# VectorE's row order, a TensorE transposition in tile 0 and the place of the second value rows, in a fused decoder layer

## What is computed

```python
x = x + _L0_attn_ref(_layernorm(x, axis=-1), L0_attn_W_qkv, L0_attn_W_out, L0_attn_b_out)
x = x + _L0_xattn_ref(_layernorm(x, axis=-1), ctx_1024, ctx_1024, mask_Bx1xSxS2_ik1, ...)
x = x + _L0_ffn_ref(_layernorm(x, axis=-1), L0_ffn_w1, L0_ffn_b1, L0_ffn_w2, L0_ffn_b2)
# self attention, in blocks of 128 rows
scores = jnp.where(causal, jnp.einsum('bnqd,bnkd->bnqk', blk(q), blk(k)) * scale, -jnp.inf)
p = jnp.exp(scores - max); p = p / (sum(p) + 1e-06); out = p @ blk(v) @ W_out.T + b_out
# cross attention
scores = jnp.where(mask == 0, NEG_INF, q @ k.T * SCALE); out = (silu(scores) @ v) @ Wo.T
```

## Time and profile before

| | before |
|---|---|
| median of 3 runs | 1257.65 us |
| profiled execution, device time | 1257.62 us |
| its span, first to last instruction | 1255.8 us |
| PE / DVE / ACT / POOL busy | 98% / 56% / 39% / 20% |
| mean granted TensorE clock | 0.994 |

### The profile page before, as it was taken

How to read it: one execution, slowest core, us unless ns; L and a number is a source line. 1 busy time by engine, 2 the same in 40 slices (tenths; PEclk the granted TensorE clock), 3 DMA queues, 4 the chain that set the end, 5 groups by cost and what they waited for, 6 DMA issues and landing times.

```text
span 1255.8 us, 15452 instructions
## 1 busy us (share of the span) xinstructions
PE 1230.2 (98%) x5560; PEld 1019.8 (81%) x5560; DVE 700.8 (56%) x1266; ACT 489.6 (39%) x888; POOL 254.1 (20%) x226
## 2 busy tenths in 40 slices
PE   9979999999999999999999999999999999999998
PEld 7867878787878788878888888888888888888887
DVE  8777878887888876855733433424424333334211
ACT  7336464646464648453332232222222222323221
POOL 2223232323232332159402001001001020010000
PEclk9999999999999999999999999999999999999999
DMA  8451515151515140325120010020100200100000
GB/s 298 148 138 33 156 35 155 33 158 36 153 34 154 38 118 13 126 92 178 50 67 1 1 68 1 1 67 0 64 3 0 67 0 0 67 0 0 35 1 33
DMA packets 76789, 82.22 MB, mean 65 GB/s; under 512 B 8257, under 2 KB 47169, under 8 KB 76737
## 3 DMA queue, kind: packets, MB, share of 16 engines
q1 hardware_dynamic: 68672, 77.90, 20.0%
q10 hardware_dynamic: 8064, 3.67, 1.3%
HBM read 48.51 MB, written 18.35 MB: 53 GB/s over the span
## 4 chain that ended last, share of the span: by engine, by line
PE 55%; DVE 0%; issue 0%; DVEq 0%
PE bank L54 18%; PE bank L55 18%; PE bank L56 18%; DVE resid L1403 0%; DVEq L1402 0%
## 5 line engine op out<-in xcount | busy, mean ns | idle before, releaser
L1393 DVE TENSOR_TENSOR hid_lo<-gelu_out,hid_hi 128x512 fp32r<-128x512 f32 x128 | 97.3, 760 | 405.0 <-ACT gelu_out L1357 405.0
L1353 ACT ACTIVATE hid_hi<-bank,small 128x512 fp32r<-128x512 f32 x128 | 88.0, 688 | 499.2 <-PE bank L56 499.2
L54 PE MATMUL bank<-zT,w_parts 128*128 128x512 f32 x656 | 255.5, 389 | 1.7 <-DVE zT L864 0.9
L56 PE MATMUL bank<-zT,w_parts 128*128 128x512 f32 x656 | 255.3, 389 | 0.0
L55 PE MATMUL bank<-zT,w_parts 128*128 128x512 f32 x656 | 255.3, 389 | 0.0
L54 PE MATMUL bank<-w2p_hi,hid_lo 128*128 128x512 f32 x512 | 199.3, 389 | 0.0
L55 PE MATMUL bank<-w2p_lo,hid_hi 128*128 128x512 f32 x512 | 199.3, 389 | 0.0
L56 PE MATMUL bank<-w2p_hi,hid_hi 128*128 128x512 f32 x512 | 199.2, 389 | 0.0
L54 PEld LDWEIGHTS bank<-zT,w_parts 128*128 128x128 f32 x656 | 123.1, 188 | 28.1 <-issue 2.6
L55 PEld LDWEIGHTS bank<-zT,w_parts 128*128 128x128 f32 x656 | 123.2, 188 | 25.4
L56 PEld LDWEIGHTS bank<-zT,w_parts 128*128 128x128 f32 x656 | 123.1, 188 | 25.5
(11 more groups left out here) (156 smaller groups left out, 2039.9 us busy)
## 6 DMA issues: line engine op xcount, KB each, us to landing
x_in<-in_x SPq DMA_DIRECT2D x32, 256.0 KB, 4.8
x_dram<-resid SPq DMA_DIRECT2D x32, 256.0 KB, 2.4
raws<-in_w SPq DMA_DIRECT2D x32, 256.0 KB, 3.2
resid<-x_dram SPq DMA_DIRECT2D x32, 256.0 KB, 3.7
out_dram<-resid SPq DMA_DIRECT2D x32, 256.0 KB, 2.1
raws<-in_x SPq DMA_DIRECT2D x28, 256.0 KB, 3.5
z_cols<-raws SPq DMA_DIRECT2D x112, 64.0 KB, 2.0
z_cols<-scratch SPq DMA_DIRECT2D x56, 64.0 KB, 2.1
```

Source lines behind the costliest of these rows:

```text
L54: pe.matmul(out_ap, lhs[1], rhs[0], start=start, stop=False)
L56: return pe.matmul(out_ap, lhs[0], rhs[0], start=False, stop=stop)
L1353: act.activation(hid[0][:, c % 4, :], bank[4 + c % 3][:, :], ACT.Gelu, bias=b1_col[:, c:c + 1])
L1393: dve.tensor_tensor(hid[1][:, c % 4, :], gelu_out[:, c % 2, :], f(hid[0][:, c % 4, :]), ALU.subtract).then_inc(hid_lo, 1)
```

## The change

It does three things, and what goes with them.

1. DVE in a step: `rows_ahead` and `mask_now` stand ahead of `start_step` in every step from 1 (the mask in step 7 too); then `q_low` 0 to 2, `values_low`, `q_low` 3. GpSimd's bias adds now wait in every step from 1 to 6 for the keys' low parts (`kv_ready`).
2. Tile 0's second normalisation is transposed by TensorE: 16 transposes into banks 7, 5, 0, 1 behind `y_rows` 1 of tile 1, evacuated by ACT and DVE. Its `turn2` and 16 DMAs go. DVE makes tile 1's z1 low parts (`z1_low`) ahead of tile 0's second statistics.
3. TensorE in a step: value rows 1 stand in front of the self scores, in step 0 too, with their wait for the third masked score.

```diff
+FIRST_Z2_BANK = (7, 5, 0, 1)
@@ sync, step
-                            if more(a):
-                                sp.wait_ge(z2_turned, NB * (a + 1))
+                            if more(a) and not first(a):
+                                sp.wait_ge(z2_turned, NB * a)
                                 move_squares(sp, scratch, range(QUADS // 2), z2_moved)
@@ gpsimd, step
-                                if b is not None and first(b):
-                                    pool.wait_ge(kv_ready, HEADS_PER_CHUNK)
+                                if b is not None:
+                                    pool.wait_ge(kv_ready, len(BLOCKS) * b + HEADS_PER_CHUNK)
@@ scalar, step
+                                if first(a):
+                                    for i in range(NB):
+                                        act.wait_ge(z2T_done, i + 1)
+                                        act.activation(attn[0][:, :, cols(i)], chunks(bank[FIRST_Z2_BANK[i]][:, :]),
+                                                       ACT.Copy).then_inc(z2T_hi, 1)
@@ vector, step
-                                if first(b):
+                                if more(a):
                                     rows_ahead(a + 1, b)
-                                    mask_now(b)
+                                mask_now(b)
                                 start_step(b)
-                                if more(a) and not first(b):
-                                    rows_ahead(a + 1, b)
-                                q_low(b, 0)
-                                q_low(b, 1)
-                                if not first(b):
-                                    mask_now(b)
-                                q_low(b, 2)
-                                if not first(b):
-                                    values_low(b)
+                                for m in range(EC - 1):
+                                    q_low(b, m)
+                                values_low(b)
                                 q_low(b, EC - 1)
                                 dve.wait_ge(mask_ready, b + 1)
                                 for j in range(3):
                                     mask_scores(b, j)
-                                if first(b):
-                                    values_low(b)
@@ vector, after the first residual
+                            if first(a):
+                                for c in range(EC):
+                                    z1_low(1, c)
@@ tensor, step
                             value_rows(0)
+                            if b is not None:
+                                pe.wait_ge(s2_masked, PAIRS * b + 3)
                             pe.wait_ge(y_lo, EC * (a + 1))
+                            value_rows(1)
...
-                            if b is not None:
-                                pe.wait_ge(s2_masked, PAIRS * b + 3)
-                            value_rows(1)
@@ tensor, y_rows of the next tile
                                 for m in range(EC):
                                     y_rows(a + 1, m)
+                                    if first(a) and m == 1:
+                                        pe.wait_ge(keys_out, EC)
+                                        for i in range(NB):
+                                            transposed_rows(pe, z2_ready, a, i, FIRST_Z2_BANK[i], z2T_done)
```

More of the change, by code:

```diff
@@ L642, in last_step @@
                         def last_step(b):
-                            sp.wait_ge(z2_moved, MOVES * (TILES - 1))
+                            sp.wait_ge(z2_moved, MOVES * (TILES - 2))
                             for c in range(STAGES):
@@ L774, in step @@
                                     z1_high_now(a + 1)
-                                act.wait_ge(z2_turned, NB * (a + 1))
-                                move_squares(act, scratch, range(QUADS // 2, QUADS), z2_moved)
+                                if not first(a):
+                                    act.wait_ge(z2_turned, NB * a)
+                                    move_squares(act, scratch, range(QUADS // 2, QUADS), z2_moved)
                                 y_high(a + 1, 0)
                                 y_high(a + 1, 1)
-                                act.wait_ge(z2_moved, MOVES * (a + 1))
-                                for c in range(EC):
-                                    act.activation(by_blocks(attn[0], c), by_quads(c), ACT.Copy).then_inc(z2T_hi, 1)
+                                if first(a):
[3 more added lines that the diff above has]
+                                                       ACT.Copy).then_inc(z2T_hi, 1)
+                                else:
+                                    act.wait_ge(z2_moved, MOVES * a)
+                                    for c in range(EC):
+                                        act.activation(by_blocks(attn[0], c), by_quads(c), ACT.Copy
+                                                       ).then_inc(z2T_hi, 1)
                                 y_high(a + 1, 2)
@@ L785, in step @@
                                 for i in range(NB):
-                                    transpose_high(act, i, BLOCK_BANK[i], z2T_done, z2T_hi, 0)
+                                    transpose_high(act, i, BLOCK_BANK[i], z2T_done, z2T_hi, 1)
                         def last_step(b):
@@ L867, in rows_ahead @@
                         def rows_ahead(n, b):
+                            if b is not None and first(b):
+                                dve.wait_ge(z2T_done, NB)
                             norm_rows(dve, lambda i: ahead[i], mv1, rstd1, ln1, n)
@@ L873, in turn2 @@
                             dve.wait_ge(z2_ready, NB * (a + 1))
-                            if b is not None:
-                                dve.wait_ge(attn_lo, PAIRS * (b + 1))
+                            dve.wait_ge(attn_lo, PAIRS * (b + 1))
                             dve.nop(nofuse=True)
@@ L999, in step @@
                             if more(a):
-                                for c in range(EC):
-                                    z1_low(a + 1, c)
+                                if not first(a):
+                                    for c in range(EC):
+                                        z1_low(a + 1, c)
                                 norm_rows(dve, lambda i: x1_rows(i, par), mv2, rstd2, ln2, a)
-                                turn2(a, b)
-                                if b is not None:
+                                if not first(a):
+                                    turn2(a, b)
                                     for i in range(3):
@@ L1015, in step @@
                                 y_low(a + 1, 1)
-                                for c in range(EC):
-                                    z2_low(a, c)
+                                if first(a):
+                                    for i in range(NB):
+                                        dve.wait_ge(z2T_hi, i + 1)
+                                        dve.tensor_tensor(attn[1][:, :, cols(i)],
+                                                          chunks(bank[FIRST_Z2_BANK[i]][:, :]),
+                                                          f(attn[0][:, :, cols(i)]), ALU.subtract).then_inc(z2T_lo, 1)
+                                else:
+                                    for c in range(EC):
+                                        z2_low(a, c)
                                 y_low(a + 1, 2)
@@ L1032, in last_step @@
                             start_step(b)
-                            dve.wait_ge(z2T_done, NB)
+                            dve.wait_ge(z2T_done, 2 * NB)
                             norm_rows(dve, lambda i: x_in[:, i, :], mv3, rstd3, ln3, 0)
```

## The result

The kernel after takes 1260.84 us (median of 10 runs, 1259.94 to 1262.19), the kernel before 1257.62 us in as many. The ratio is 1.0024, 95% interval 1.0015 to 1.0034: 3.2 us slower. That is small, but the interval leaves out a ratio of 1. The forecast was 1258.6 with a range of 1253.5 to 1262.5.

The account below looks back on a forecast made before the run. TensorE, busy 1230.2 of 1255.8 us, was taken as the bound. Terms -3.1 - 1.9 - 1.9 + 1.9 + 2.5 = -2.5 us, -0.9 with step 0's low clock, +1.9 for drops at new waits: +1, 1258.6 us, range 1253.5 to 1262.5.

Parts of the forecast that it names:

- The new waits of 1.6 us at the softmax transposition: TensorE at L1161: profile to show about 1.45 us in each of steps 1 to 7, 3.3 in step 0.
- Front halves of 35.2: A step's first query to first PV matmul: 35.2 us, bounds 34.8 to 35.8; before, 32.34 to 36.15 in steps 2 to 7.
- the overlap with GpSimd: On VectorE, the first `values_low` meets GpSimd's last add and takes 0.4 us more, bounds 0 and 1.0.
- The third masked score: On VectorE, the three masked scores end at Q + 16.15, Q being the step's first query matmul.
- TensorE's wait at value rows 1: In a step, 0.9 us waited for the third masked score instead of 2.15; shown as 0.7 at L54.
- Step 0: PV +2.7 us, low clock 1.6 more; TensorE transposes bring step 1's queries to 90.76 without low clock, -3.1 net.
- The clock at the new waits: L1161 in steps 1 to 7: one or two clock drops in seven, at most 1.25 us each, +1.9 us.
- behind PV nothing changes: From PV to the next queries it is TensorE's own work, 27.2 us, unchanged.
- A: Rival: value rows are cover that isn't missed, softmax chain does not bind; 1238 us, chance 4%.
- B: Rival: clock stays up and no `values_low` overlap with GpSimd; 1252.8 to 1255.1 us, chance 13%.
- C: Rival: clock falls at L1161 waits in steps 1 to 7, 1.25 us each; 1260.5 to 1265.5 us, chance 28%.
- D: Rival: step 0's new path isn't ready, rows or evacuation late; adds 0 to 1 us, no separate chance given.

Follow-up runs that it names:

- third run: Kernel after with value rows 1 behind the self scores again in every step (parts 1 and 2 kept), 44 added TensorE waits: 1233.21 us, ratio 0.9802.
- fourth run: Kernel after with 40 added waits, value rows 1 behind the self scores in steps 0 and 7 only: 1249.57 us, ratio 0.9931.
- last run: Kernel after with 40 added waits, GpSimd's new wait for the keys' low parts undone in steps 2 to 6: 1275.91 us, ratio 1.0146.
- first run: Kernel after, placed: 40 long-met wait instructions added on TensorE in step 0's last y_rows, nothing else: 1256.28 us, ratio 0.9985.
- second run: Kernel before with 37 added TensorE wait instructions, its feed-forward loop beginning as far into the code as in the kernel after: 1261.23 us, ratio 1.0022.
- eighth run: Kernel before with parts 1 and 2, value rows 1 behind the self scores, without the 44 added waits: 1237.13 us, ratio 0.9838.
- seventh run: Kernel before with part 3 alone, value rows 1 in front of the self scores: 1283.13 us, ratio 1.0202.
- part 1 alone: Kernel before with only VectorE's new order and GpSimd's wait for the keys' low parts: 1242.35 us, ratio 0.9882.

## Why the prediction was right, and where it was not

**The new waits of 1.6 us at the softmax transposition: right.** The wait is shown as 1.26 to 1.35 us in seven steps and 3.16 in step 0; 1.45 and 3.3 were foretold. In the kernel after, the chain from the self scores' end to masked score 7 is again 12.44 us in step 7 (489.77 to 501.53 + 0.68; VectorE's timeline):

```profile
501.53 0.68 DVE L859 SCALAR_TENSOR_TENSOR scratch<-bank,mask_i 128x512 f32<-128x512 f32 x1
```

The third run shows that the value rows were the cover: behind the self scores again, the front halves fall to 32.34.

**Front halves of 35.2: right, 0.2 too long.** The failing piece is the overlap with GpSimd. The third masked score was put at Q + 16.15 and came at Q + 15.90 (168.87 + 1.89 - 154.86). `values_low` took 1.35 us, 0.11 over its 1.24, not 0.4:

```profile
165.93 1.35 DVE L910 TENSOR_TENSOR vb_lo<-values_now,vb_hi 64x128 fp32r<-64x128 f32 x4
168.87 1.89 DVE L859 SCALAR_TENSOR_TENSOR scratch<-bank,mask_i 128x512 f32<-128x512 f32 x3
```

GpSimd's last add ended at 166.18, only 0.25 us behind its start. For the same reason TensorE's wait at value rows 1 is shown as 0.25 to 0.39 us in six steps, where 0.7 was foretold. The contention itself was no mistake: with GpSimd's adds early it costs 15 to 20 us in all.

**Step 0: right, in part by luck.** PV at 71.31 (69.75 + 1.6 expected), step 1's queries at 92.51 (91 to 92), the low clock behind the 3.16 us wait at the price of 1.56. The fourth run, with the wait back at its old length, has neither. But the low clock does not follow each time: in the last run (GpSimd's adds early on the first run's kernel) the same wait of 3.17 us stands ahead of the same matmuls, and they took 3.22 us at full clock instead of 4.83.

```profile
67.32:70.54 3.22, 3.22 (x17) 1.00 0.89 223
```

Four of the eleven executions of the first run have a mean clock of 1.000 and took 1255.3 to 1255.7 us, the other seven 0.999 and 1256.3 to 1256.8. That fits a drop in seven of eleven. The 1.6 us of this term thus come by chance, though more often than not.

The 16 transposes took 1.67 us (85.27 to 86.94), so the 104 ns of the trace of before held. By the figure of about 275 ns in Part 4 of the Trainium skill's "TensorE: Matmul & The Clock Gate" an estimate would have made it 4.4.

**The clock at the new waits: wrong.** I had taken one or two drops in the seven waits of about 1.3 us, 1.9 us, and there was none: all seven front halves ran at 1.00. The chance that it gave this term failed, not the size of a drop. Without the term the steps were to gain 0.9 us, and they gained 0.5.

**Behind PV: one wait overlooked.** In step 3 the queries waited 1.21 us for `attn`, whose moves in step 2 ended over 1 us later than in the placed kernel. The cover there was 0.1 to 0.5 us, which the prediction's "behind PV nothing changes" did not count. The moves of the ACT queue, in the kernel after and in the first run:

```profile
205.54 6.86 ACTq L263 DMA_DIRECT2D z_cols<-scratch  x8
205.96 5.20 ACTq L274 DMA_DIRECT2D z_cols<-scratch  x8
```

Among the moves of the kernel after lies an instruction packet (q8, at 209.5 us, 1.6 us long), and none among those of the first run. In the twelve traces together there are 76 such sets of eight moves on the ACT queue. 73 of them take 5.2 to 5.6 us; the other three take 6.86, 6.64 (second run) and 5.87 (eighth run), and these three alone have a q8 packet begin among them. So this wait too goes with the place of the code and not with the change: the second run, whose steps are those of before, has it with 0.99 us. That the packet delays the moves is argued from this, not tested by itself.

**The feed-forward part: missed.** The sum took it as unchanged, and it lost 3.5 us (703.43 instead of 699.92 from its first matmul to the end of the span). This was no term and no rival: the prediction had no place in it for where code lies. It is larger than the net of all that the steps changed. The forecast of 1258.6 came as near as 2.2 us by luck, since two errors partly met: 1.9 us of clock that did not come, and 3.5 of pauses that were not in the sum. Of the sum, 0.9 under before for the steps was right to 0.4 us.

**The rivals.** A (value rows not needed as cover) falls with the third and the seventh run. B was half right, for the seven later waits. C did not decide: no drop at 1.3 us. D did not come: the new path was in time.

**The parts nearly add up.** Alone, part 1 is worth 14.8 us, part 2 7.3, in all 22.1; together (third run) they are worth 24.7 against its own median of before, 1257.91. Of the 2.6 between, 1.9 is the longer step 4 behind VectorE's pause in part 1 alone; the rest is no more than the groups of runs differ by. Part 3 alone costs 26.0, and 23.1 on top of the others. The change is a gain of some 24 us with a loss of the same size in it, and the pauses on top.

## What to carry to other kernels

Independent work that stands between a producer and a long chain's consumer is cover. Before moving it ahead of the producer, add up what is left between the two and set it against the chain (here 4.54 of 6.15 us). Undo each part of a change by itself: this one reads as "no difference" and holds a version 2% faster. And when a loop far from the edit gets slower, look for waits that nothing releases and for instruction packets early in each later round, and try the same kernel with a few instructions more ahead of it.

## What the runs showed of the hardware that I had not expected

- TensorE's loop over two feed-forward tiles either runs without instruction packets from its second round (kernels that begin it 0, 4 or 77 instructions later than before) or fetches 16 to 18 of them between 800 and 1150 us and pauses 0.7 to 1.8 us early in each later round (33 or 37 instructions later, three kernels). Timed, that is 3.3 us on the kernel before (1257.91 to 1261.23), 4.6 on the kernel after and 3.9 on the third run's; the last two are between groups of runs, and part of them is the wait of step 3.
- The traces say more on this than the runs were made for. Counting TensorE's instructions, a q8 packet of 16 KB comes once for every 256 of them, as if the code were cut in stretches of that length. If a stretch begins where its packet is seen to start, the loop begins 209, 213 or 30 instructions into one in the kernels without pauses, and 242 or 246 in those with them. A round has 1574 instructions, so it lies in seven stretches in the first case and in eight in the second. An estimate from this: seven are kept for the next round, eight are not, and the kernel before was 9 instructions short of the eighth. Five starting places fit it; no run was made to test it.
- After TensorE waits of 1.25 to 1.38 us, and after the pause of 1.76, the clock stayed up every time; after 1.84 to 1.99 us it fell in some steps and not in others with the same wait; after 2.4 us in two of five; after 2.86 to 3.10 in three of five; after 3.16 to 3.17 in step 0 in three kernels of four; after 4.9 to 6.2 ahead of step 1's queries each time.
- Some VectorE instructions take longer beside GpSimd's adds: four of the keys' low parts (two SBUF inputs) 4.83 us instead of 1.76, the mask (one) 1.56 instead of 0.43. Others do not: a half of `q_low`, which reads PSUM too, takes 0.74 to 0.76 us beside them and away from them. When GpSimd's adds start, beside these instructions or behind them, was worth 15 to 20 us, though they share no data.
